# Recurrent layer kernel, second attention: the value sums of a group in one step instead of three

## What is computed

```python
def _attention(x, wq, wk, wv, wo):
    B, S, D = x.shape
    q = (x @ wq).reshape(B, S, N_HEADS, HEAD_DIM).transpose(0, 2, 1, 3)
    k = (x @ wk).reshape(B, S, N_KV_HEADS, HEAD_DIM).transpose(0, 2, 1, 3)
    v = (x @ wv).reshape(B, S, N_KV_HEADS, HEAD_DIM).transpose(0, 2, 1, 3)
    ...
    scores = jnp.einsum('bhqd,bhkd->bhqk', q, k) / jnp.sqrt(jnp.float32(HEAD_DIM))
    scores = jnp.where(causal, scores, -jnp.inf)
    attn = jax.nn.softmax(scores, axis=-1)
    out = jnp.einsum('bhqk,bhkd->bhqd', attn, v)
    return out.transpose(0, 2, 1, 3).reshape(B, S, D) @ wo
```

## Time and profile before

| | us |
|---|---|
| median of 3 runs | 3356.93 |
| lowest and highest | 3354.94, 3363.76 |
| the profiled execution | 3356.11 |
| its span | 3354.3 |
| TensorE busy in the span | 3130.9 (93%) |
| VectorE, ScalarE, GpSimd busy | 2236.8, 2052.0, 1164.7 |
| value sums (L2094) | 1024 of 23170 matmul records, from 2283.5 to 2711 us |

### The profile page before, as it was taken

One profiled execution on the slowest core, in us unless ns is written; L12 is line 12 of the kernel. 1 busy time (PEld: TensorE's weight loads), 2 busy tenths in 40 slices (PEclk: granted clock), 3 DMA queues, 4 the chain that ended last, 5 costly groups with the idle time before them and its releaser, 6 DMA issues. The chain is left out here.

```text
span 3354.3 us, 75760 instructions
## 1 busy us (share of the span) xinstructions
PE 3130.9 (93%) x23170; PEld 2393.5 (71%) x23170; DVE 2236.8 (67%) x6696; ACT 2052.0 (61%) x4941; POOL 1164.7 (35%) x1836
## 2 busy tenths in 40 slices
PE   4999999999999999989999996969999974999995
PEld 3676777767767677768888884536666664999995
DVE  5888888888888888876656664547766726333334
ACT  4777777777777777765565553316666643333333
POOL 4444444444444444443333330034232202333331
PEclk9999999999999999999999998979999976999998
DMA  3111111111111111134333332111111133223225
GB/s 89 34 36 33 26 35 36 36 33 36 36 33 36 36 35 34 36 112 139 125 128 116 132 125 70 44 50 29 35 40 42 42 99 115 39 37 88 39 37 170
DMA packets 143913, 208.80 MB, mean 62 GB/s; under 512 B 29762, under 2 KB 101826, under 8 KB 143778
## 3 DMA queue, kind: packets, MB, share of 16 engines
q1 hardware_dynamic: 130914, 189.46, 18.8%
q0 software_dynamic: 12864, 17.57, 3.2%
HBM read 123.22 MB, written 39.98 MB: 49 GB/s over the span
## 5 line engine op out<-in xcount | busy, mean ns | idle before, releaser
L770 POOL TENSOR_SCALAR at_p<-at_p,at_recip 128x512 f32<-128x512 f32 (+3 forms) x1030 | 536.6, 539 | 824.6 <-DVE at_recip L917 824.6
L826 ACT ACTIVATE at_p<-at_p,at_nmax 128x512 f32<-128x512 f32 (+3 forms) x1032 | 570.5, 555 | 130.4 <-DVE at_nmax L911 124.0
L911 DVE CUSTOM_DVE_ANT_0 at_p<-at_s_ps,at_bias 128x512 f32<-128x512 f32 (+3 forms) x1032 | 462.1, 488 | 63.2 <-PE at_s_ps L1043 44.5
L1043 PE MATMUL at_s_ps<-at_k_twice,at_q 64*128 64x512 f32 (+3 forms) x3096 | 341.8, 340 | 3.1 <-DVE at_nmax L911 3.1
L1902 DVE CUSTOM_DVE_ANT_0 aa_a_ps<-aa_a_ps,aa_hidden 128x128 f32<-128x128 f32 (+3 forms) x512 | 242.3, 512 | 118.4 <-PE aa_a_ps L2066 116.2
L1065 PE MATMUL at_o_ps<-at_pT,at_v 128*64 128x512 f32 (+3 forms) x2064 | 306.5, 439 | 0.0
L923 DVE COPY at_pT<-at_t_ps 128x512 f32<-128x512 f32 (+3 forms) x512 | 239.0, 488 | 94.1 <-PE at_t_ps L1055 90.2
L1802 ACT ACTIVATE aa_pT<-aa_b_ps 128x512 f32<-128x512 f32 (+1 forms) x384 | 197.4, 529 | 145.3 <-PE aa_b_ps L2084 139.1
L1055 PEld LDWEIGHTS at_t_ps<-ident,at_p 64*128 64x128 f32 x5120 | 189.2, 138 | 120.3 <-issue 120.3
L449 ACT ACTIVATE nw_h<-nw_h_ps,nw_b 128x512 f32<-128x512 f32 x192 | 132.2, 689 | 210.9 <-PE nw_h_ps L553 210.4
L526 DVE SCALAR_TENSOR_TENSOR nw_hl<-nw_h,nw_coef_now,nw_hh 128x512 fp32r<-128x512 f32 x192 | 150.1, 782 | 163.9 <-ACT nw_hh L454 163.9
(11 more groups left out here) (307 smaller groups left out, 7772.4 us busy)
## 6 DMA issues: line engine op xcount, KB each, us to landing
at_k_twice<-at_k_twice SPq DMA_DIRECT2D x130, 256.0 KB, 2.8
nw_w_raw<-in_w_all_dram SPq DMA_DIRECT2D x26, 1024.0 KB, 5.1
nw_w_raw<-in_w_all_dram SPq DMA_DIRECT2D x52, 512.0 KB, 6.9
w_all<-in_w_dram SPq DMA_DIRECT2D x12, 768.0 KB, 10.1
nw_xh<-xh_dram SPq DMA_DIRECT2D x10, 512.0 KB, 4.3
nw_xl<-xl_dram SPq DMA_DIRECT2D x10, 512.0 KB, 5.0
at_w_raw<-in_w_heads_dram SPq DMA_DIRECT2D x18, 256.0 KB, 3.8
nw_x<-in_x_dram SPq DMA_DIRECT2D x9, 512.0 KB, 6.0
```

The source lines that it names most:

```text
L770: pool.tensor_scalar(p, p, recip[:, u:u + 1], 1.0, ALU.mult, ALU.mult).then_inc(scaled, 1)
L826: act.activation(p_sb[:, u, 0:N], p_sb[:, u, 0:N], ACT.Exp, bias=nmax[:, u:u + 1], scale=-1.0, accum_out=total[:, u:u + 1]).then_inc(exped, 1)
L911: dve.tensor_tensor_reduce(out=p_sb[:, u, 0:N], in0=s_ps[u % 2][:, score_at(u // 2)], in1=bias[:, u % 2, S - N:S], scale=1.0, scalar=BIG, ...
L1043: ins = pe.matmul(s_ps[h][:, score_at(j)], qst[par][rows, q, at], k_twice[par][rows, k, 0:N], start=(i == 0), stop=(i == 2))
```

## The change

In the loop, all four blocks of group G - 1 now stand in the step with h = 1, behind the 384-column score and ahead of the third piece. The steps with h = 0 and h = 2 hold none.

```diff
--- before.py
+++ after.py
@@ -2149,16 +2149,12 @@
                     if ahead:
                         score(G + 2, h, 2)
                     if h == 1 and G > 0:
-                        weigh(G - 1, 1)
-                    if h == 2 and G > 0:
-                        weigh(G - 1, 2)
-                        weigh(G - 1, 3)
+                        for k in range(TT):
+                            weigh(G - 1, k)
                     piece(n, s, 2)
                     if ahead:
                         score(G + 2, h, 3)
                     side(side_job(n, s, 1))
-                    if h == 0 and G > 0:
-                        weigh(G - 1, 0)
             for k in range(TT):
                 weigh(GROUPS - 1, k)
             for half in range(2):
```

## The result

| | before | after |
|---|---|---|
| median of 22 runs each, us | 3355.76 | 3360.91 |
| lowest and highest | 3353.24, 3363.76 | 3358.16, 3364.33 |
| the profiled execution, its span | 3356.1, 3354.3 | 3363.1, 3361.3 |
| second attention's loop, first piece to first piece of the last step | 440.70 | 444.80 |

The ratio is 1.0015 (95%: 1.0009 to 1.0022): slower by 5 us, inside the 0.3% that I called no change, but a real difference and not the 0.1 us of the forecast. It is as large as the -5 to +5 that my errors allowed if all went one way. Of the 7.0 us between the two spans 3.3 lie ahead of the loop, where both kernels are the same (over the twelve traces the loop starts between 2263.6 and 2267.7), and 4.1 in the loop (and -0.4 behind it). The rest of the text is about these 4.1.

A forecast was written before the change was run, and what follows sets the result against it. TensorE bounds the kernel on average, with thin buffers (two b banks). Six middle batches save 2.7 us and give back 2.7, the first adds 0.4, the last -0.3: 0.1 on 3356.9 gives 3357, range 3343 to 3370.

The forecast's parts named there:

- what a change over costs: TensorE, into and out of the 32-column sums: some 0.3 us each, 0.67 saved a group, 20.8 over 31 groups.
- Full gain: Rival: ScalarE's stops are not as walked, saved change overs remain; -10 with half given back, -21 (3335) with none; chance 0.16.
- ScalarE gives back most of it: Steps that lose sums wait for ScalarE's exponentials; a batch gives back 2.7 us and saves 2.7.
- s10 to s12: Three of a batch's sixteen steps, s0 to s15: ScalarE's queue walked start to start makes them 7.9, giving back 1.1.
- s14 and s15: Last two steps of a batch: ScalarE's queue makes them 4.4, the next s0's transposes wait 0.1 more; 0.5 given back.
- s4 and s5: First spread's 1.07 stop for VectorE's split stays, exponential waits behind k's copies; 0.76 given back, together +1.1.
- VectorE has room: VectorE's masks start after their scores as before; its 39.83 us busy of 57.83 a batch leave room.
- the clock: Named as a sign of being wrong, if it falls in a stop; the batch was to stay within 0.6 of 57.8.
- the ends: First batch saves in three groups only, +0.4; last batch has no next batch's jobs, -0.3 estimated.
- s7 and s0, s8: s7's output projection waits for VectorE's operand, s6 and s7 giving back about 0.35; s0 and s8 give the full 1.19.
- the sign that I named: Idle of weight loads before pieces, put down to ScalarE's exponentials, should rise by 15 to 20 us.
- Starvation: Rival: ScalarE starves in newly unweighted s0, s2, s4, s6, s8, losing 0.4 each, +2 a batch, 3371; chance 0.18.

The follow-up runs named there:

- one-part runs: Against the kernel before: only block 0 moved from h = 0 to h = 1, 0.9993; only blocks 2 and 3 moved from h = 2 to h = 1, 1.0021.
- the run with fewer copies: Second copy of each spread k left out from the third batch on, both kernels with the early split: changed kernel 0.9951, kernel before 0.9972.
- blocks 2 and 3 moved alone: Kernel before with only blocks 2 and 3 moved from h = 2 to h = 1, block 0 left at h = 0: 1.0021, loop 448.98.
- block 0 alone: Kernel before with only block 0 moved from h = 0 to h = 1, blocks 2 and 3 left at h = 2: 0.9993, loop 439.96.
- two stretches: Changed kernel with the third piece put between blocks 1 and 2, same step: 1.0033, loop 454.62.
- all at h = 2: Changed kernel with all four blocks in the step with h = 2 instead of h = 1: 1.0029, loop 451.15.
- copies by VectorE: Changed kernel with both copies of each spread k by VectorE instead of ScalarE from the second batch on: 1.0030, loop 450.83.
- the early split: VectorE's split of k put ahead of taking v in step 3: changed kernel 0.9984, kernel before 0.9988, block 0 alone 0.9975.

## Why the prediction was right, and where it was off

**Right: what a change over costs.** 0.67 us a group from two fewer. The step with h = 1 grew by 1.50 to 1.52 wherever nothing else is on the path (1.51 forecast), and cutting the stretch once costs 0.27. Full gain, my first rival, did not come.

**Right: ScalarE gives back most of it, in s5, s10 to s12, s14 and s15.** s10 to s12 7.89 (7.9 forecast, and ScalarE's rows follow the walk start by start), s14 and s15 4.45 (4.4 from the queue, 4.5 with the transposes' wait). The one-part runs show it by absence (s10 without its sums is not shorter), the run with fewer copies by cause.

**Off: the stop in s4.** I wrote that the first spread's stop "stays". It grew from 1.07 to 1.34, and s4 and s5 came to +1.39 instead of +1.08. The mis-sized term is VectorE's split, which I took as a fixed duration that moves with its place. Groups view of the split, before (least, median and greatest in ns):

```profile
L1890 DVE TENSOR_TENSOR aa_kk<-aa_turn,aa_kk x8: 685/1060/1370, 2226.0 to 2625.0; 64x512 fp32r<-64x512 f32 x8
```

and after:

```profile
L1890 DVE TENSOR_TENSOR aa_kk<-aa_turn,aa_kk x8: 684/1326/1334, 2228.8 to 2631.0; 64x512 fp32r<-64x512 f32 x8
```

In n = 2 it lasts 0.27 longer (1.06 to 1.33) since it now meets another of GpSimd's operations, and this is the size of the plain middle batch's +0.27. My sentence that VectorE has room, by its busy time, looked at the wrong thing: its split and its product each depend on what GpSimd is doing when they start. In n = 3 it went the other way: 1.37 before, 0.91 after, s4 1.35 shorter, but s7 0.61 longer.

**Off: the clock.** I named it as what would make me wrong and gave it no term. It fell twice in the loop after, in n = 4 and n = 5, never before; these two batches last 58.83 and 58.75, outside the 57.8 by 0.6 that I had set. The window of the first fall:

```profile
2515.60:2519.00 3.40, 3.40 (x15) 2.96 (x14) 2.71 (x13) 2.54 (x5) 3.16 (x4) 0.50 0.04 7
```

and TensorE ahead of it and in it, in the timeline:

```profile
2514.91 0.47 PE L2027 MATMUL aa_m_ps<-aa_kk,aa_spread 128*128 128x512 f32 x1 [1.34 <-DVE aa_kk L1890]
...
2515.63 0.52 PE L2066 MATMUL aa_a_ps<-aa_k,aa_q 128*128 128x384 f32 x1
...
2517.87 1.05 PE L2040 MATMUL aa_m_ps<-ident,aa_minus 128*8 128x128 f32 x4
```

3.4 us at a granted clock of 0.50, which is 1.2 GHz, from 0.7 us behind the stop of 1.34 on; the second fall begins 0.1 us before its stop ends. These two batches cost 0.7 more than the plain ones. The other runs say the same: the clock granted over the whole program is 0.9669 in the mean of the 22 runs after and 0.9681 to 0.9683 in those of the kernel before on three chips, a difference of two to three such falls (an estimate: 3.4 us at half clock are 0.0005 of 3360 us). With blocks 2 and 3 moved alone a fall cost 2.4: 1.5 in s4, where it meets a step with sums and full pieces, and 0.9 in s7, where TensorE then waits 0.64 for VectorE's product. s4 of its n = 1, with a fall, and of its n = 2, without:

```profile
2336.38:2342.53 6.15, 4.80 (x23) 2.45 (x22) 4.55 (x13) 2.65 (x5) 5.66 (x7) 0.72 0.20 47
2397.18:2401.78 4.60, 3.26 (x22) 1.92 (x21) 4.27 (x13) 2.11 (x4) 4.27 (x5) 1.00 0.25 59
```

**Off: the ends.** The first batch came to +0.72 (+0.4 forecast), since its s8 is only 0.90 shorter; the last to +0.53 (-0.3), since its steps without sums shorten by 5.6 in all and the four with h = 1 grow by 6.1. So the loop's 4.1 is 0.1 as forecast, 0.3 and 0.8 for the ends, 1.4 for the clock, 1.3 for the longer split in five batches and 0.1 for n = 3.

**Off, without effect: s7 and s0, s8.** The output projection gave back 0 in five of six middle batches, not 0.25: VectorE's product was over in time, except in n = 3 (1.51 long, s7 +0.61). s0 and s8 gave 1.07 and 1.09, not 1.19. They nearly cancel, which is luck: the 0.1 us that is "as forecast" in the loop's 4.1 is a sum of such misses.

**Wrong: the sign that I named.** The idle of weight loads put down to exponentials was to rise by 15 to 20 us. Waits view over the loop (us, count, greatest), before:

```profile
ACT aa_pT L1802 <- PE aa_b_ps L2084: 139.1, 150, 1.9
...
PEld aa_b_ps L2081 <- ACT aa_pT L1802: 51.6, 103, 0.8
...
PE aa_b_ps L2081 <- ACT aa_pT L1802: 3.3, 11, 0.3
```

and after:

```profile
ACT aa_pT L1802 <- PE aa_b_ps L2084: 152.1, 150, 2.5
...
PEld aa_b_ps L2081 <- ACT aa_pT L1802: 34.8, 81, 1.2
...
PE aa_b_ps L2081 <- ACT aa_pT L1802: 10.7, 24, 0.8
```

It fell by 17. A weight load waits for the exponential in many steps in which TensorE is still busy with the matmul before, and I take it that these harmless waits went with the steps' new shape; no run tests that. Those that count are the idle of the matmul itself, which rose from 3.3 to 10.7, and TensorE's idle in the windows, up 10.7.

**Starvation**, the slower rival, did not come in its form: s0, s2, s6 and s8 gave up at most 0.12 each, not 0.4. s4 gave up 0.3 apart from its stop (n = 0, where the stop kept its length, is 0.88 shorter, not 1.19), and 0.2 of that was in the forecast.

**Still open.** Why the clock falls in or behind some stops and not others. In the six loops with the split at its old place (after, block 0 alone, blocks 2 and 3 alone, two stretches, all at h = 2, copies by VectorE) it fell 16 times up to the last batch's last step, each time in s4 or within 0.1 us of s5's start. In the five loops with the early split it never did. The kernel before has stops of 1.07 to 1.38 and no fall; block 0 alone fell behind one of 1.08. So the falls belong to the stop for the split, but its length doesn't tell which. Why s8 of the first batch gives less is open too, and so is what all four blocks at h = 2 would do without the stop.

## What to carry to other kernels

A merge of work that needs a mode of its own saves what each change of mode costs, here 0.3 us, only if the engine that feeds the bottleneck through few buffers (here two) is not next in line. Before it, count the feeder's queue over each stretch that loses the work, start to start, against the bottleneck's arrival: a move from a stretch with slack (block 0 out of s8, blocks 2 and 3 out of s2) keeps nearly all it saves, one from a stretch without (blocks 2 and 3 out of s10) is given back whole. Judge by distances between starts and by the matmul's own idle, not by the weight loads' idle; and when a moved stop hangs on an elementwise operation, look at what runs beside it at the new place.

## What the runs showed of the hardware

**VectorE and GpSimd hold each other up.** An operation of VectorE with two SBUF operands that starts while GpSimd is in one of its own ends 0.54 to 0.55 behind the end of that one, wherever it started. In the twelve traces' loops the split and the product do so all 134 times that they last over 0.70; in the 20 cases in which GpSimd was within 0.15 of its end they last their usual 0.69. The split after, n = 2:

```profile
2396.65 1.26 POOL L1773 TENSOR_TENSOR aa_turn<-aa_turn 128x512 f32<-128x512 f32 x1
...
2397.13 1.33 DVE L1890 TENSOR_TENSOR aa_kk<-aa_turn,aa_kk 64x512 fp32r<-64x512 f32 x1
...
2398.00 0.94 POOL L1775 TENSOR_SCALAR aa_q_parts<-aa_turn 64x512 fp32r<-64x512 f32 x1
```

GpSimd ends at 2397.91, the split at 2398.46. GpSimd's next one takes 0.94, and the like one behind it 0.65. With the early split in the changed kernel, the product of the output projection:

```profile
2402.11 1.29 POOL L1773 TENSOR_TENSOR aa_turn<-aa_turn 128x512 f32<-128x512 f32 x1
...
2402.41 1.54 DVE L1928 TENSOR_TENSOR aa_oT<-aa_o_packed,aa_shares 128x512 f32<-128x512 f32 x1
...
2404.01 0.48 PE L2050 MATMUL aa_m_ps<-aa_wo,aa_oT 128*128 128x256 f32 x1 [0.36 <-DVE aa_oT L1928]
```

Ends at 2403.40 and 2403.95. Alone both take about 0.69. In the kernel before with the early split, the split starts 0.07 behind the start of the same GpSimd operation and lasts 1.75, of which 0.54 lie behind the end of GpSimd's. The Trainium skill, "SBUF — State Buffer", section "SBUF: two separate sides", says that an instruction of VectorE with two SBUF inputs and one of GpSimd that reads SBUF take a shared port pair as an exclusive lock. The trace agrees: the loser waits, and does not merely run slower, since the time behind the other's end is the same 0.54 to 0.55 for an overlap of 0.2 or of 1.2 us.
